# Moving the LayerNorm sums of a fused Mamba and FP4 kernel to ScalarE, with every engine's jobs in a new order

## What is computed

```python
def _layernorm(x, axis=-1, eps=1e-05):
    m = jnp.mean(x, axis=axis, keepdims=True)
    v = jnp.var(x, axis=axis, keepdims=True)
    return (x - m) / jnp.sqrt(v + eps)
...
    x = x + _L0_attn_ref(_layernorm(x, axis=-1), ...)
    x = x + _L0_ffn_ref(_layernorm(x, axis=-1), ...)
```

## Time and profile before

| | |
|---|---|
| median of three runs | 4461.37 us |
| the profiled execution | 4469.2 us, of which its span is 4467.1 us |
| busy share of the span | DVE 96%, POOL 91%, PE 90%, ACT 77% |
| granted TensorE clock, mean | 0.992 |
| moved by DMA | 739 MB, 165 GB/s |

### The profile page before, as it was taken

The page is one execution under the profiler, slowest core; times in us unless marked ns, Lnnn a source line. Parts: engine busy times, 40 slices in busy tenths (PEclk is TensorE's granted clock), DMA queues, the critical chain, the costliest instruction groups (busy, mean ns, idle before and its releaser), DMA issues. The chain is left out here.

```text
span 4467.1 us, 64797 instructions
## 1 busy us (share of the span) xinstructions
PE 4032.4 (90%) x18416; PEld 1950.3 (44%) x18732; DVE 4284.4 (96%) x6316; ACT 3450.3 (77%) x5783; POOL 4043.1 (91%) x2833
## 2 busy tenths in 40 slices
PE   3789999999999999999999999999999999999987
PEld 1234444444444444444444444444444444444435
DVE  6999999999999999999999999999999999999994
ACT  3778878877877878878877877878878777878763
POOL 5999999999999999999999999999999999999983
PEclk8999999999999999999999999999999999999999
DMA  3555555555545555555555545555545555555540
GB/s 90 187 174 177 169 166 177 170 166 176 172 166 176 172 166 176 172 166 175 173 166 174 173 166 174 173 166 174 174 166 173 173 167 172 174 168 170 171 157 21
DMA packets 288969, 739.06 MB, mean 165 GB/s; under 512 B 35686, under 2 KB 87014, under 8 KB 288614
## 3 DMA queue, kind: packets, MB, share of 16 engines
q1 hardware_dynamic: 286912, 732.75, 49.8%
q10 hardware_dynamic: 1702, 2.16, 0.2%
HBM read 709.61 MB, written 25.17 MB: 164 GB/s over the span
## 5 line engine op out<-in xcount | busy, mean ns | idle before, releaser
L684 POOL TENSOR_TENSOR prod<-state,cs 128x1024 f32<-128x1024 f32 x1024 | 2419.2, 2362 | 294.7 <-DVE state L920 286.1
L899 DVE TENSOR_TENSOR db<-db,du 128x512 f32<-128x512 f32 x1536 | 1044.8, 680 | 84.3 <-PE db L973 56.9
L988 PE MATMUL ybank<-prod,ident 64*64 64x512 f32 x4096 | 999.9, 606 | 72.5 <-DVE hh L849 70.7
L481 ACT ACTIVATE decay<-delta,aneg 128x512 f32<-128x512 f32 x1536 | 1049.4, 712 | 3.9 <-DVE state L920 3.8
L988 PE MATMUL cross<-prod,ident 64*64 64x512 f32 x4096 | 999.9, 607 | 0.0
L920 DVE TENSOR_TENSOR_SCAN state<-decay,carry,db 128x512 f32<-128x512 f32 x768 | 958.6, 1255 | 0.0
L920 DVE TENSOR_TENSOR_SCAN state<-decay,db 128x512 f32<-128x512 f32 x768 | 914.5, 1198 | 0.1
L481 ACT ACTIVATE db<-delta,aneg 128x512 f32<-128x512 f32 x512 | 350.6, 685 | 481.7 <-DVE state L920 481.6
L675 POOL TENSOR_TENSOR brow<-brow,du 128x512 f32<-128x512 f32 x512 | 649.6, 1269 | 0.0
L973 PE MATMUL db<-pieces,sel 128*128 128x512 bf16 x1288 | 493.0, 384 | 163.1 <-DVE state L920 161.0
L988 PEld LDWEIGHTS ybank<-prod,ident 64*64 64x64 f32 x4096 | 254.5, 133 | 473.2 <-issue 435.4
(11 more groups left out here) (128 smaller groups left out, 7172.7 us busy)
## 6 DMA issues: line engine op xcount, KB each, us to landing
cs<-c_rows SPq DMA_DIRECT2D x1024, 512.0 KB, 3.7
brow<-b_rows SPq DMA_DIRECT2D x512, 256.0 KB, 3.8
xin<-in_hidden SPq DMA_DIRECT2D x128, 128.0 KB, 4.0
xres<-in_hidden SPq DMA_DIRECT2D x128, 128.0 KB, 4.0
out_x<-ot SPq DMA_DIRECT2D x128, 128.0 KB, 3.8
c_rows<-xdbl SPq DMA_DIRECT2D x128, 32.0 KB, 3.6
b_rows<-xdbl SPq DMA_DIRECT2D x128, 32.0 KB, 3.3
win<-in_win_t SPq DMA_DIRECT2D x1, 1024.0 KB, 10.6
```

The costliest lines, as they stand in the source:

```text
L481: act.activation(out, delta[:, gu % 2, :], ACT.Exp, scale=aneg[:, gu % HEADS, gn:gn + 1]).then_inc(done, 1)
L684: pool.tensor_tensor(prod[:, r, :, :], state[:, 2 * p:2 * p + 2, :], cs[:, c, :, :], ALU.mult).then_inc(weighted, 1)
L899: dve.tensor_tensor(t[:, :], t[:, :], du[:, gu % 2, :], ALU.mult).then_inc(db_done, 1)
L988: last = pe.matmul((ybank, cross)[k][c * Q:(c + 1) * Q, :], ident[rows, rows], prod[rows, p % P_RING, k, :], start=(p == 0), stop=(k == 1 ...
```

## The change

It does four things.

- The sums of both LayerNorms come from ScalarE. A `Copy` of the tile onto itself writes the row sum (L617, L655 after the change). The centring then uses scale -256 and the sum as bias, which gives 256 times (mean - x). A `Square` with scale 256 to the power -0.5 writes the sum of squares (L558, L568). VectorE's four instructions for each unit go.
- Epsilon is no longer added: the centred tiles have a 257th column that holds a constant chosen so that its square adds epsilon's share.
- One `pow` on GpSimd serves both LayerNorms: 128x2 numbers in place of two adds and two powers of 128x1.
- Nearly all jobs get another slot, or another place in the code of their step, on all five engines. The turning of the gate and up weights moves from after units -3 and -2 to after unit -1. DMA issues, their number and their sizes stay; the waits ahead of the writes of C and B rows take in two more semaphores.

The core of the diff:

```diff
+EPS_COL = DM * (EPS * DM) ** 0.5
...
-        PLACE_AFTER = {-3: W_GATE, -2: W_UP, 0: W_DOWN}
+        PLACE_AFTER = {-1: (W_GATE, W_UP), 0: (W_DOWN,)}
...
+                if t := due("norm", -6):
+                    act.wait_ge(ld_x[t.mod(2)], t.div(2, 16, 16))
+                    wait(act, centred1, t.val())
+                    x = xin[:, t.mod(2), 0:DM]
+                    act.activation(x, x, ACT.Copy, accum_out=sum1[:, :]).then_inc(sum1_done, 1)
...
+                if t := due("norm", 2):
+                    act.wait_ge(centred1, t.val(plus=1))
+                    wait(act, rstd_done, t.val())
+                    act.activation(xin[:, t.mod(2), :], xn[:, t.mod(2), :], ACT.Square, scale=DM ** -0.5,
+                                   accum_out=ve[:, 0, 0:1]).then_inc(var1_done, 1)
...
+                if t := due("post", 18):
+                    act.wait_ge(centred2, t.val(plus=1))
+                    act.wait_ge(var1_done, min(t.val(plus=12), TILES))
+                    act.wait_ge(rstd_done, t.val(plus=11))
+                    act.activation(xin[:, (t.val() + 1) % 2, :], v2_eps[:, :], ACT.Square, scale=DM ** -0.5,
+                                   accum_out=ve[:, 1, 0:1]).then_inc(var2_done, 1)
...
+                if t := due("post", 17):
+                    act.wait_ge(sum2_done, t.val(plus=1))
+                    wait(act, v_tp, t.val())
+                    act.activation(v2, x1[:, t.mod(4), :], ACT.Identity, bias=sum2[:, 0:1],
+                                   scale=-float(DM)).then_inc(centred2, 1)
...
+                if t := due("post", 16):
+                    act.wait_ge(x1_done, t.val(plus=1))
+                    wait(act, centred2, t.val())
+                    x = x1[:, t.mod(4), :]
+                    act.activation(x, x, ACT.Copy, accum_out=sum2[:, :]).then_inc(sum2_done, 1)
...
-                pool.tensor_tensor(ve[:, 0:1], mv[:, 1:2], epsc[:, :], ALU.add).then_inc(rs, 1)
-                wait(pool, rs, t.val(2, 1))
-                pool.tensor_tensor(ve[:, 1:2], ve[:, 0:1], minus_half[:, :], ALU.pow).then_inc(rs, 1)
...
+                if t1:
+                    pool.wait_ge(var1_done, t1.val(plus=1))
+                    wait(pool, xn_done, t1.val())
+                if t2:
+                    pool.wait_ge(var2_done, t2.val(plus=1))
+                    wait(pool, v_done, t2.val())
+                which = slice(0 if t1 else 1, 2 if t2 else 1)
+                pool.tensor_tensor(ve[:, which, 1], ve[:, which, 0], minus_half[:, which],
+                                   ALU.pow).then_inc(rstd_done, 1)
...
-                    dve.bn_stats(stats2[:, :], x1[:, t.mod(4), :]).then_inc(st2, 1)
-                if t := due("post", 18):
-                    dve.bn_aggr(mv2[:, :], stats2[:, :]).then_inc(st2, 1)
...
-                    dve.bn_stats(stats1[:, :], xin[:, t.mod(2), :]).then_inc(st1, 1)
-                if t := due("norm", 4):
-                    dve.bn_aggr(mv1[:, :], stats1[:, :]).then_inc(st1, 1)
```

More of the change, by code:

```diff
@@ L430, in step @@
[L430 to L443, removed]
+                if w := due("scan", 4):
+                    spread_c(w, 3)
@@ L484, in step @@
             def step(b, j, n):
                 u, due = timetable(b, j, n)
[L486 to L495, removed]
@@ new lines, in turn_h @@
+            def turn_h(t, part):
+                pe.wait_ge(h_quant, t.val(plus=1))
+                if part == 1:
+                    pe.wait_ge(ht_done, t.val(2, 1))
+                elif (t + 2).within(TILES):
+                    pe.wait_ge(vt_done, t.val(plus=3))
+                else:
+                    wait(pe, h_op, 2 * TILES)
+                    wait(pe, ht_done, t.val(2))
+                for k in range(3):
+                    last = pe.transpose(bank_b[:, k * P:(k + 1) * P],
+                                        hh[:, t.mod(2), (3 * part + k) * P:(3 * part + k + 1) * P],
+                                        ident[:, :])
+                last.then_inc(h_tp, 1)
@@ new lines, in gate @@
+            def gate(t, part, ks):
+                for k in ks:
+                    if k > 0:
+                        pass
+                    elif part == 1:
+                        pe.wait_ge(silu_g, t.val(2, 1))
+                    else:
+                        pe.wait_ge(vt_done, t.val(plus=1))
+                        if (t + 1).within(TILES):
+                            pe.wait_ge(x1_done, t.val(plus=2))
+                        else:
+                            wait(pe, o_done, t.val(plus=-2))
+                    last = pe.matmul(bank_a[:, 0:HALF], vt[:, k, :], wg[:, k, part * HALF:(part + 1) * HALF],
+                                     start=(k == 0), stop=(k == KM - 1))
+                if k == KM - 1:
+                    last.then_inc(gu_mm, 1)
@@ new lines, in project @@
+            def project(t, heads):
+                i = t.mod(4)
+                if heads[0] == 0:
+                    pe.wait_ge(yg_done, t.div(4, 4, 4))
+                    if (t + 6).within(UNITS):
+                        pe.wait_ge(sz_done, t.val(plus=7))
+                    else:
+                        wait(pe, o_done, t.val(plus=-3))
+                for h in heads:
+                    last = pe.matmul(bank_a[:, 0:DM], yg[:, t.mod(8) // 4, h, i * P:(i + 1) * P],
+                                     wo[:, h, :], start=(h == 0), stop=(h == HEADS - 1))
+                if h == HEADS - 1:
+                    last.then_inc(op_mm, 1)
@@ new lines, in side @@
+                if w := due("scan", 1):
+                    spread_b(w.val(NST, 3))
+                if w := due("scan", 17):
+                    sum_up(w, (4,))
+                if t := due("post", 38):
+                    up(t, 1)
+                if t := due("post", 27):
+                    pe.wait_ge(v_quant, t.val(plus=1))
+                    if peeled and t.val() == 0:
+                        pe.wait_ge(xnt_done, 11)
+                    else:
+                        wait(pe, h_op, t.val(2))
+                    for k in range(KM):
+                        last = pe.transpose(bank_b[:, k * P:(k + 1) * P], v2_eps[:, k * P:(k + 1) * P], ident[:, :])
+                    last.then_inc(v_tp, 1)
```

813 lines of the change are left out of this document (439 added, 374 removed).

## The result

The changed kernel takes **4568.85 us** (median of four runs, 4559.53 to 4570.75); the kernel before, run beside it on the same chip, 4461.01 us. The ratio is 1.0235, 95% interval 1.0222 to 1.0248: slower by 2.4%, where 4414 us were predicted.

A forecast was written before the change was run, and what follows sets the result against it. VectorE (DVE), busy 96%, was taken to bound the kernel. A unit: 31.39 + 1.55 + 0.10 = 33.04 us, saving 0.37 x 128 = 47 us: 4422 against the profiled execution, 4414 us as median; range 4310 to 4468 for 8 in 10.

The forecast's parts named there:

- DVE alone: VectorE's own work in a unit, without locks: 33.41 - 0.82 - 0.56 - 0.23 - 0.41 = 31.39 us.
- The LayerNorms' 0.82: VectorE's `bn_stats` (0.33) and `bn_aggr` (0.08), both twice a unit, go: 0.82 us saved.
- the stop of 0.56: VectorE's wait for a late PE row ahead of the product at 2526.70: taken as gone, bounds 0 to 0.56 us.
- the gap of 0.23: VectorE's gap ahead of the output sum L868: taken as gone, bounds 0 to 0.23 us.
- The stops in the other units: VectorE's 0.56 us stop and 0.23 us gap, read in one unit, were taken as gone in all 128.
- The chain to `vs`: Residual sum through ACT, power and POOL's second weigh holds VectorE's scale `vs` until 13.30 us: lock 1.55 us, before 0.41.
- The scale `hs`: VectorE's scale of 128x44, near the end of POOL's weigh of states 10 and 11: 0.1 us more, bounds 0 to 0.3.
- All units taken as one: One unit of 33.41 us, between two residual sums on VectorE, stood for all 128: 4276 us, 191 us for start and tail.
- The start: Turning gate and up in one piece ahead of the first scan: taken as 0, bounds -5 to +10 us once.
- The slower side: Rival: longer chain at POOL's one power behind the second square; unit 33.97 us, total time 4533 us; chance 0.14.
- the signs that I named for being right: No `bn` groups; residual sums 32.5 to 33.3 us apart; `vs` near 1.7; power within 0.1 of square; state 6 stop gone.
- The load of a table: ACT's table load in the chain takes 1.28 us by the row; the skill's drain would add 1.38 us a unit.

## Why the prediction was wrong

- **DVE alone: right, in the unit that I read.** 31.39 us were predicted without any lock; the short unit of 33.02 less its two locks (1.69 - 0.16 and 0.27 - 0.16) is 31.38. The LayerNorms' 0.82, the stop of 0.56, the gap of 0.23: gone there, as said.
- **The stops in the other units: mis-sized.** I took 0.79 us as gone from every unit, 101 us. DVE's idle time inside the full units of before was 72 us in all (a mean of 0.69 us in units without carries, 0.49 in units with them), and 43 us are left (0.26 and 0.44).
- **The chain to `vs`: right.** Second square at its end 7.84 us after the residual sum's start (7.97 predicted), DVE at `vs` after 11.73 (11.59), its end after 13.42 (13.30). Some terms were off and nearly cancelled. An accumulating output costs 0.09 and not 0.15, but the instruction that it belongs to takes 0.30 to 0.33 and not 0.27. From the end of the square to the power are 0.23 us and not 0.08, and the power of two numbers takes 0.65 to the next start and not 0.51. In units with carries `vs` is cheaper, 1.05 to 1.46, since DVE comes later; the mean of all is 1.33 where 1.71 was counted, 48 us to the good.
- **The scale `hs`: the step that failed.** I gave it "Bounds 0 to 0.3; I take 0.1", since "it arrives about 0.3 before that end, but no reciprocal waits right behind it". In the units without carries it arrived 0.2 before that end, and cost 0.1 in 53 of them but 2.4 in 7, in which it stood through the next weigh as well. In the 60 units with carries that take 2.2 it arrived 0.15 after that end, at the start of the next weigh, and cost 2.1. The mean is 1338 ns against 163, thus 1.17 us a unit, 150 us in all, where 13 were counted. Two things were missed in this one bound. POOL has its next weigh ready there, so the far end of the bound is the rest of the running instruction plus the whole next one, 2.6 us, and not 0.3. And a forecast 0.3 us from the edge of a step must hold for every kind of unit.
- **All units taken as one: the reason behind it.** The earlier trace rows is a unit without carries, and 128 x 33.41 was my sum. Units with carries have 16 scans of 0.06 us more, 0.96 in all; the trace of before has most of them at 33.6 to 33.8, only 0.3 longer, because they waited and stood less (0.49 idle and 0.26 in `vs`, against 0.69 and 0.53). So they had about 0.46 us less to save, and against POOL's phase their scans shift DVE by the 0.3 us that decide.
- **A count: wrong, without effect.** SP issues 17 transfers a unit before and after, not 14; no term of the sum hangs on it.
- **The start: mis-sized.** Bounds -5 to +10, measured -30.1 us. Without this luck the result would have been 4599.
- **The rivals.** The slower side came, but not by the mechanism that I gave it (a longer chain through the power, 0.14). The range ended at 4468, too low by 101 us. The same lock, which I had read from the trace and priced at `vs`, decided at `hs`. Of the signs that I named for being right, the mean of `vs` and the distance of the residual sums fail in the units with carries, and the power starts 0.23 us behind the square, not 0.1.
- **The load of a table: right.** The chain came out 0.13 us below the sum that was made with the row's 1.28 us for the load. The 1.38 us more that the Trainium skill gives (ScalarE: Activation LUTs, section What ACT_TABLE_LOAD costs) are not in it.

## What to carry to other kernels

An instruction of VectorE that POOL can hold has a price that jumps with its phase: near zero at the end of POOL's instruction, and nearly all of the next one when it comes 0.3 us later. Bound it by POOL's running instruction plus what is ready behind it, in every kind of unit, not in the one that was read. A better slot gave back 266 us here, but its gain hangs on the phase. An engine that isn't held gave more: 60 numbers a row moved to ACT took 327 us off, and made the slower kernel 5% faster than the old one.

## What was not expected of the hardware

- A held instruction of DVE doesn't always get its turn at the end of the POOL instruction that holds it. With back-to-back instructions on POOL it got in at the first change in some units and stood on in others of the same run. In the changed kernel, 2.11 to 2.14 us into a weigh, 53 units got in and 7 stood through one more (2.6 us). With `hs` moved alone, 1.50 to 1.54 us into it, 42 got in and 18 stood through two more (4.41 us). With `vs` on ACT, 36 of 37 units that came 1.94 to 1.99 us into it stood through one more (2.75 us). In the longest case it ended when POOL itself was waiting. What decides between them no view of the trace shows, and it stays open; no run here was made for it.
- A `SCALAR_TENSOR_TENSOR` with both inputs in SBUF is held like a `TENSOR_SCALAR` between SBUF tiles (1351 and 1425 ns mean); a `RECIPROCAL` between SBUF tiles isn't (240 and 398 ns).
- An accumulating output of ACT is an instruction of its own, 0.18 to 0.20 us long, that costs 0.09 us to the next start.
